# New order tables for five engines, with a due time of its own for every patch step and every group

## The reference, cut to what matters

```python
pe = conv(x, conv_w, stride=14)                 # 9x9 patches of 256 channels
red = mean over each 3x3 window; win = its 9 cells
q = ln(red) @ wq; k, v = ln(win) @ wkv          # 8 heads, softmax over the 9 cells
local_out = red + agg @ proj + b                # 9 tokens per image
cls_out = class_emb + attention of one query over local_out
patch_out = local_out @ mod_w + mod_b
h = concat([patch_out, cls_out, txt])           # 64 x 87 x 256
q, k, v = ln(h) @ w_qkv                         # 16 heads of 16
q, k = rope(qk_norm(q), qk_norm(k))             # norm over the head's 16
h = h + softmax(q k^T / 4) v @ w_proj + b
x = ln(h); s = softmax(x @ gate_w.T)            # 8 experts, top 2
h = h + x @ W_lin.T + b + sum_top2(s * x @ left @ right)
```

## Time and profile before

| what | before |
|---|---|
| median of 3 runs | 742.79 us (741.1 to 745.35) |
| span of the profiled execution | 734.0 us |
| PE busy | 673.9 us, 92% |
| DVE, POOL, ACT busy | 531.2, 491.0, 432.0 us |
| chain that ended last | PE 71%, DVE 12%, ACT 4%, issue 4%, SPq 3%, POOL 3%, DMA 2% |

### The profile page before, as it was taken

How to read it: one execution, slowest core, us unless ns; L and a number is a source line. 1 busy time by engine, 2 the same in 40 slices (tenths; PEclk the granted TensorE clock), 3 DMA queues, 4 the chain that set the end, 5 groups by cost and what they waited for, 6 DMA issues and landing times.

```text
span 734.0 us, 24407 instructions
## 1 busy us (share of the span) xinstructions
PE 673.9 (92%) x9431; PEld 564.8 (77%) x9431; DVE 531.2 (72%) x1192; ACT 432.0 (59%) x1115; POOL 491.0 (67%) x564
## 2 busy tenths in 40 slices
PE   5998998999985799999999999999999999999873
PEld 3987887888853577888888888888888888887652
DVE  2468687887978646788878878878878887866642
ACT  4553452635442346677777676677776777776541
POOL 3667563764648428787877877876976977975442
PEclk9999999999996969999999999999999999999996
DMA  8963472231011223223232332332332332122001
GB/s 222 237 163 116 129 224 47 54 83 44 22 24 40 59 54 79 63 70 82 67 78 73 75 83 73 79 82 72 78 83 68 79 86 67 42 54 62 26 25 34
DMA packets 69528, 58.73 MB, mean 80 GB/s; under 512 B 30607, under 2 KB 68646, under 8 KB 69286
## 3 DMA queue, kind: packets, MB, share of 16 engines
q1 hardware_dynamic: 69414, 57.18, 30.9%
HBM read 33.69 MB, written 11.40 MB: 61 GB/s over the span
## 4 chain that ended last, share of the span: by engine, by line
PE 71%; DVE 12%; issue 4%; ACT 4%; SPq 3%; POOL 3%; DMA 2%; POOLq 0%; DVEq 0%; ACTq 0%
PE p_a L1355 13%; PE p_c L1355 10%; PE p_conv L758 8%; PE p_kv L758 7%; PE p_o L1427 6%; PE p_s L1415 5%; PE p_mm L758 4%; PE p_s L1397 4%; PE p_n L1435 3%; PE p_c L1474 3%; PE p_a L1381 3%; PE p_s L1411 2%; DVE t L1282 2%; DMA kr<-qkT 2%; DVE kv L656 1%
## 5 line engine op out<-in xcount | busy, mean ns | idle before, releaser
L1291 DVE TENSOR_REDUCE mx<-p_s 87x16 bf16<-87x1392 f32 x64 | 102.5, 1602 | 44.6 <-PE p_s L1397 44.4
L1214 ACT ACTIVATE prT<-p_s 87x1392 f32<-87x1392 f32 x64 | 85.2, 1331 | 29.3 <-PE p_s L1415 27.8
L1121 POOL TENSOR_TENSOR t<-t,ss_rs 116x512 f32<-116x512 f32 x48 | 50.9, 1060 | 58.9 <-ACT ss_rs L1190 57.8
L426 POOL TENSOR_TENSOR xs_lo<-xcols,xs_hi 120x585 fp32r<-120x585 f32 (+1 forms) x45 | 60.4, 1348 | 43.7 <-ACT xs_hi L483 43.7
L1415 PE MATMUL p_s<-qr,kr 32*87 32x87 f32 x2048 | 68.8, 257 | 0.0
L1115 POOL TENSOR_TENSOR t<-t 116x512 f32<-116x512 f32 x48 | 62.4, 1299 | 5.6 <-DVE t L1282 5.6
L1135 POOL TENSOR_TENSOR yT_lo<-y_raw,yT_hi 128x232 fp32r<-128x232 f32 x48 | 32.5, 678 | 47.1 <-issue 31.4
L1124 POOL TENSOR_TENSOR t<-t,tabs 116x512 f32<-116x512 f32 x48 | 61.2, 1276 | 2.7
L1415 PEld LDWEIGHTS p_s<-qr,kr 32*87 32x87 f32 x2048 | 60.3, 154 | 0.0
L1411 PE MATMUL p_s<-mxT,pick_row 32*87 32x87 bf16 x1024 | 55.7, 208 | 1.9 <-ACT mxT L1208 1.9
L1427 PE MATMUL p_o<-prT,vp 87*32 87x87 f32 x2048 | 55.1, 248 | 0.1
...
## 6 DMA issues: line engine op xcount, KB each, us to landing
...
```

What stands on the lines that cost most here:

```text
L426: nc.gpsimd.tensor_tensor(xs.lo[:, n % XS_SLOTS, :, 0:M].bitcast(F32R), raw, xs.hi[:, n % XS_SLOTS, :, 0:M], ALU.subtract).then_inc(S['xs_ ...
L1214: nc.scalar.activation(prT[:, k % 2], p_s[0:SEQ, :, 0:QUADS * SEQ], ACT.Exp, scale=HD ** -0.5).then_inc(S['s_exp'], 1)
L1291: nc.vector.reduce_max(mx[:, k % 2, :, 0:QUADS], p_s[0:SEQ, :, 0:QUADS * SP].rearrange("p j (a k) -> p j a k", k=SP)[:, :, :, 0:SEQ], AX_X ...
```

## The change

`play` takes its starts from two lists in place of two products, and all ten tables are new, with times in ns. The steps in the tables are the same ones, with the same counts; no instruction is added or removed by the tables. One POOL step, the first `hb`, gets two waits more.

```diff
 def play(windows, window_step, groups, group_step):
-    turns = [(WINDOW_PERIOD * s + time, window_step, name, s, k) for s in range(STEPS) for name, k, time in windows]
-    turns += [(GROUP_START + GROUP_PERIOD * g + time, group_step, name, g, k) for g in range(GROUPS) for name, k, time in groups]
+    turns = [(WINDOW_AT[s] + time, window_step, name, s, k) for s in range(STEPS) for name, k, time in windows]
+    turns += [(GROUP_AT[g] + time, group_step, name, g, k) for g in range(GROUPS) for name, k, time in groups]
...
-WINDOW_POOL = table("""xlo.0.-120 xlo.1.-71 xlo.2.-39 xlo.3.2 xlo.4.16 red.1.31 red.2.40 xlo.5.86 red.3.101 red.4.110 xlo.6.118
-                xlo.7.133 xlo.8.194 red.5.209 red.6.221 red.7.258 red.8.275 vw.0.551 vw.1.566 vw.2.582""")
-WINDOW_PERIOD = 403
+WINDOW_POOL = table("""xlo.0.-5901 xlo.1.-5724 xlo.2.299 xlo.3.3420 red.1.9820 xlo.4.11351 xlo.5.11807 red.2.15345 xlo.6.17419
+                red.3.17516 red.4.22961 xlo.7.23086 xlo.8.25273 red.5.27333 red.6.33268 red.7.33653 red.8.34313
+                vw.0.58996 vw.1.60160 vw.2.67521""")
+WINDOW_AT = (-2651, 37754, 78919, 119493, 159822)
...
-GROUP_SP = table("""cols.0.-400 rows.0.-440 place.0.210 values.0.258 place.1.291 values.1.438 store.0.1111 store.1.1115 store.2.1253""")
-GROUP_PERIOD, GROUP_START = 276, 2100
+GROUP_SP = table("""cols.0.-63160 rows.0.-46935 place.0.2191 values.0.22610 place.1.25097 values.1.26261 store.0.93771
+                store.1.106453 store.2.114162""")
+GROUP_AT = (210114, 237680, 265329, 292897, 320326, 347981, 375495, 403100, 430654, 458073, 485772, 513403, 541004,
+            568650, 596093, 623691)
...
                     if g == 0 and k == 0:
                         pool.wait_ge(W['agg'], STEPS)
                         pool.wait_ge(consts.S['rope_in'], 48)
+                        for part in range(2):
+                            pool.wait_ge(W[f'st_rows{part}'], ROWS_OUT * len(range(part, STEPS, 2)))
```

More of the change, by code:

```diff
@@ L266 @@
-WINDOW_SP = table("""x.0.-398 x.1.-317 x.2.-245 rows.0.736 cls.0.970""")
-WINDOW_PERIOD = 403
+WINDOW_ACT = table("""xhi.0.-11715 xhi.1.-7239 xhi.2.-1331 pe.0.2939 pe.1.4298 xhi.3.5890 xhi.4.6541 xhi.5.7215 xT.0.9051 pe.2.9341
+                xhi.6.10116 xT.1.10381 pe.3.11080 xhi.7.11205 xT.2.11482 pe.4.11643 kv.0.12938 xhi.8.12939
+                xT.3.15752 pe.5.18376 pe.6.21292 xT.4.21307 kv.1.21520 xT.5.21953 kv.2.24073 pe.7.27696
+                xT.6.28369 pe.8.28673 kv.3.29395 xT.7.30392 kv.4.30833 red_rs.0.30853 kv.5.37488 redT.0.39746
+                xT.8.40204 kv.6.43734 kv.7.45072 kv.8.46849 rstd.0.47359 exp.0.51304 aggT.0.65229 loT.0.70162
+                lo_rs.0.78876 patT.0.79362 g_exp.0.83831 ga.0.89634""")
@@ new lines @@
+WINDOW_PE = table("""conv.0.-4698 conv.1.-3301 xT.0.1125 conv.2.5659 conv.3.7114 xT.1.7357 conv.4.10215 kv.0.10594 xT.2.10884
+                conv.5.11734 kv.1.12143 xT.3.12402 xT.4.13781 conv.6.15134 kv.2.15507 conv.7.17600 kv.3.21027
+                xT.5.22078 xT.6.22251 conv.8.23831 kv.4.27729 xT.7.27732 kv.5.28664 kv.6.30341 redT.0.34371
+                xT.8.35034 q.0.35687 kv.7.36878 kv.8.38262 aggT.0.63526 proj.0.67467 loT.0.68654 mod.0.69356
+                patT.0.73349 gv.0.73794 gT.0.76490 gB.0.86719 ga.0.88208 cl.0.90173""")
@@ L906, in patch_tokens @@
     return sync, gpsimd, scalar, vector, tensor, S
[L909 to L921, removed]
@@ L922 @@
-GROUP_POOL = table("""xc.0.-264 xlo.0.-86 add.0.33 scale.0.63 shift.0.110 add.1.153 scale.1.166 shift.1.177 add.2.220 scale.2.249
-                shift.2.260 hb.0.571 oB_lo.0.599 hb.1.582 oB_lo.1.683 oB_lo.2.688 oB_lo.3.768 hb.2.612
-                yT_lo.0.856 yT_lo.1.880 yT_lo.2.925 base.0.931 above.0.969 base.1.1036 base.2.1070""")
-GROUP_SP = table("""cols.0.-400 rows.0.-440 place.0.210 values.0.258 place.1.291 values.1.438 store.0.1111 store.1.1115 store.2.1253""")
-GROUP_PERIOD, GROUP_START = 276, 2100
+GROUP_ACT = table("""xhi.0.-12313 rstd_a.0.-5771 sq.0.-2823 sq.1.2657 rstd_r.0.3945 v.0.7058 v.1.8121 qkT.0.10579 rstd_r.1.12761
+                sq.2.13549 qkT.1.17060 rstd_r.2.19950 v.2.21108 qkT.2.27292 mT.0.30131 exp.0.33544 mT.1.34915
+                exp.1.37763 oT.0.39347 mT.2.41373 exp.2.43682 oT.1.45972 mT.3.51189 exp.3.54620 oT.2.56653
+                oB.0.57214 oB.1.62023 oT.3.63064 oB.2.63780 oB.3.71738 yT.0.75185 yT.1.77492 rstd_c.0.85558
+                ffn.0.86390 ffn.1.89188 yT.2.89344 ffn.2.91393 gate.0.97638 twT.0.109509""")
```

22 lines of the change are left out of this document (added).

## The result

The changed kernel takes **782.31 us** (median of 5 runs, 774.17 to 796.33) against 742.79 (740.7 to 745.62): ratio 1.047, interval 1.040 to 1.055, so 5% slower. The forecast was 748.0 with a range of 738 to 760, so it has the sign and misses the size by 34 us.

The account below looks back on a forecast made before the run. The prediction took PE, 92% busy, as the bound, with the loop through ACT's copy and place.0 level with it. Terms +7.7 (group loop), −1.1 (window stage) and −1.5 (transition) made +5.1 on 742.8: forecast 748.0, range 738 to 760.

Parts of the forecast that it names:

- Step e: SP queue: place.1 starts later behind 3 to 4 us more issuing, lands 0.7 us before peak.2; priced at 0.
- D: Rival, much slower: place.1 lands too late for peak.2, period 29.9, +22 us, 762 us in all; chance 0.10.
- E: Clock rival: PE's added waits are 0.6 us and spread out, so no cost of clock; given no chance.
- Steps a to d: Group stage, PE, ACT and SP's place.0: loop through ACT's qkT.1 copy lengthens the period to 28.80 us, +7.7 in all.
- The loop through ACT's copy and `place.0`: From peak.0 through ACT's qkT.1 copy and place.0's DMAs to the next peak.0: 28.05 us before, 28.80 after.
- step c: ACT: exp.2 starts 0.33 us later and oB.3 now follows it, so the qkT.1 copy ends 0.75 us later.
- a: PE: mT.2 and scores.2 become adjacent, nothing covers ACT's copy of the maxima; +0.33 us a period.
- b: PE: more work ahead of proj.1 removes its wait for h2.0, −0.19 us; PE's own period becomes 28.3.
- Step g: Window stage: loT and patch waits hidden, −3.8; redT copy +0.7, aggT and vw.2 +2.0; sum −1.1 us.
- Step h: Transition to the groups: a POOL window product moves behind shift.0, −1.5 us; new waits on hb.0 priced at 0.
- the 8.8 us between span and median: Added to the profiled execution's 734.0 us to give the median, 742.8, to which the terms were added.
- The Trainium skill's formula for one DMA: Alternative landing estimate for place.0, 2.13 us for 2.4: period 28.5, term +3.8; not adopted.

Follow-up runs that it names:

- cols_values: Kernel before with store.0, cols, values.0, store.1 between place.0 and place.1 on SP, rows and store.2 staying behind place.1: 739.32 us, ratio 1.002.
- store2_front: cols_values with store.2 (a group later) right behind place.0, so SP's whole new order but rows: 743.71 us, ratio 1.003.
- sp_new: Kernel before with SP's new order alone and the two new waits in POOL's first hb: 777.29 us, ratio 1.048.
- sp_pool_old: Changed kernel with the order of before on SP and POOL, all other engines in the new order: 765.83 us, ratio 1.035.
- rows_ahead: Changed kernel with POOL's hb.1 and hb.2 at their old places and SP's rows behind place.1, loading the group after: 750.76 us, ratio 1.012.
- mod_cover: Kernel before with kv.5 and kv.6 moved ahead of mod and patT in PE's window table: 742.31 us, ratio 0.999.
- after_again: The changed kernel itself, run once more unchanged: 784.96 us, ratio 1.055.

## Why the prediction was wrong

**Step e failed, in the term of its issue times.** It said "3 to 4 us more of issuing", so a start at about 5 us and a landing 0.7 us before `peak.2`, priced at 0. (Its list of what stands ahead isn't quite the new order: `values.0` and `store.0` stood there before, and `store.1` is missing.) The start is at 8.02 in group 8, and `peak.2` waits: the prediction's own sign of being wrong. The missing 3 us are `cols` and `values.0`, 1.87 and 4.80 us behind the 348 KB of `rows`, where the step's sum leaves room only for the 0.95 and 2.7 that they take elsewhere. With those (cols_values, store2_front) `place.1` starts at 4.0 to 4.3, and the price is 0, as step e had it.

**The rival that came true is D**, with its place (`place.1` for `peak.2`) and nearly its point ("later than 5.5 us"; the runs have it near 6). It was priced at a period of 29.9, 762 us in all, and is 30.98 and 782; part of that is clock, which E had put at nothing, since the small waits of before left it at 1.00. The waits of the changed kernel are longer (up to 3.4 us for `vp`), and three groups ran at 0.90. The Trainium skill ("TensorE: Matmul & The Clock Gate", section "HAM oscillation — how this bites in real kernels") tells of a kernel in which waits for a DMA, longer than nearly all here, bring the clock down to half each time. This trace agrees in part: the clock fell behind waits of 2.0 to 2.5 us in groups 4 to 6, and stayed at 1.00 with one of 2.50 in group 12. The forecast should have given D's waits a chance of costing clock. D's chance of 0.10 was too small for a term whose cover was 0.7 us of slack on an estimate of eight issue times.

**`values.0` was not followed to its reader.** Step e looked at `place.1` alone; `pv.0` waits for `vp` 19.3 us in all. How much of it is a loss of its own isn't separated; little, by sp_new, where the waits for `vp` are 4.2 us and the period is only 0.4 shorter.

**Steps a to d, the forecast's own mechanism, were too dear.** The loop through ACT's copy and `place.0` is there (waits for `kr` at `peak.0` of 0.31 and 0.81 us in sp_pool_old), but the copy ends 0.38 us later, not 0.75. Most of the difference is that `exp.2` starts 18.38 us behind `peak.0` (522.59), as early as before (18.35), where step c had moved it by a's 0.33; the rest is that the copy begins while `oB.3` still runs. The period without SP's part is 28.31 (sp_pool_old) to 28.66 (rows_ahead), so the term is +1.3 to +5.8, not +7.7; the kernels with only SP's order changed and the time of before have 28.24 to 28.59, so it can hardly be told from nothing. `scores.2` waits 0.32 us behind `mT.2`, as a said (0.33), and PE's waits for `h` went, as b said, but PE's own period became no longer by it: 27.9 to 28.1 in the periods of sp_pool_old that don't end in such a wait, not 28.3.

**Step g: the sign of the parts was right, the sum not.** The waits for `loT` and `patch` went; mod_cover shows that this gains nothing. A new wait came that g had not seen, 7.4 us in all for `pT_lo`, whose low part DVE makes behind the reduction of `agg` (DVE, then PE, in the first profile of the changed kernel):

```profile
154.68 2.77 DVE L691 TENSOR_REDUCE agg<-kv 117x256 f32<-117x1536 f32 x1
...
159.25 0.37 DVE L639 TENSOR_TENSOR pT_lo<-p_xT,pT_hi 128x234 fp32r<-128x234 f32 x1
```

```profile
159.77 0.75 PE L762 MATMUL p_kv<-w_kv_hi,pT_hi 128*117 128x512 f32 x1 [4.35 <-DVE pT_lo L639]
```

`peak.0` of group 0 starts at 248.40 in after_again and at 251.61 in the first profile, against 248.01 before: window stage and transition came out at +0.4 to +3.6, where g and h had −2.6. One profile tells this badly: kernels with the window tables of before (SP's aside) have 248.0 to 249.5 here, those with the new ones 248.4 to 252.2, some 1.5 more on the mean and not 2.6 less.

**Step h: the new waits in `hb.0` are not free on POOL**, 7.5 us once:

```profile
POOL hb L1159 <- DMA h_tokens<-cls_out: 7.5, 1, 7.5
```

In the kernels with all other engines in the order of before the same waits are there and the time is that of before (cols_values, mod_cover), so there they cost nothing that shows. How much of the changed kernel's head they make was not separated. With `rows` moved away (rows_ahead) 9.5 us over the kernel before remain, by the spans 10.2 in the head and 5.8 in the 13 periods, less what the profile of before was shorter than its median. In after_again the head's part lies in groups 0 and 1: 66.6 us, with waits of 1.32 for `kr` and 3.36 for `vp`, against 56.6 before. Which move makes it longer stays open.

**One reading of the times was off**: the 8.8 us between span and median do not lie around the span. The changed kernel's runs lie 1.7 us above their spans (784.96 is a median, but 792.59 has a span of 790.9), so the profiled execution of before was itself some 7 us faster than the median. It changed no term of the forecast, but differences of spans to it come out larger than those of medians: 48.1 us against 40 to 44.

The Trainium skill's formula for one DMA ("DMA: Bandwidth & Descriptors", section "Anatomy of one DMA — SWDGE (gpsimd) path") would have given a period of 28.5. That is nearer to what runs without `rows` in front show (28.24 to 28.66) than the 28.80 of the sum, but by luck: what made the sum too long was the end of the copy, not the landing. It wasn't the term that mattered.
